# A fused two-layer window-attention kernel: VectorE's order within a slot rewritten, and v taken out of its bank by one operation per half

## What is computed

```python
qkv = (xw @ qkv_w + qkv_b)            # xw: (windows, 64 tokens, 192)
q, k, v = ...                         # 12 heads of 16
attn = softmax(q @ k.T * scale [+ bias + mask])
out = attn @ v                        # per window and head
x = shortcut + unshift(out @ proj_w + proj_b)
x = x + gelu(layernorm(x) @ fc1_w + fc1_b) @ fc2_w + fc2_b
```

## Time and profile before

| | us |
|---|---|
| median of three runs | 4492.06 (4489.7 to 4493.99) |
| the profiled execution, its own time | 4490.49 |
| its span, from first to last instruction | 4488.7 |
| mean granted TensorE clock | 0.904 of 2.4 GHz |
| TensorE matmul busy | 3937.7 (88%) |
| VectorE busy | 3454.4 (77%) |
| GpSimd busy | 3358.2 (75%) |
| ScalarE busy | 2729.8 (61%) |

### The profile page before, as it was taken

The page is one execution under the profiler, slowest core; times in us unless marked ns, Lnnn a source line. Parts: engine busy times, 40 slices in busy tenths (PEclk is TensorE's granted clock), DMA queues, the critical chain, the costliest instruction groups (busy, mean ns, idle before and its releaser), DMA issues. The chain is left out here.

```text
span 4488.7 us, 170135 instructions
## 1 busy us (share of the span) xinstructions
PE 3937.7 (88%) x62800; PEld 2783.4 (62%) x62800; DVE 3454.4 (77%) x9093; ACT 2729.8 (61%) x5921; POOL 3358.2 (75%) x6257
## 2 busy tenths in 40 slices
PE   3888988988999899899889889998998898898888
PEld 2556666666666666666666666666666666666665
DVE  5777777777777777777777777777777777777776
ACT  1566666666666666666666666666666666666665
POOL 4777777777777777777777777777777777777775
PEclk9899998999899899989989998998999899899899
DMA  4877887887788688778867877887787788678775
GB/s 101 148 136 143 143 140 140 141 143 140 138 144 141 137 142 144 136 141 142 142 139 140 142 140 140 141 145 137 143 141 137 142 140 144 141 142 138 135 134 101
DMA packets 2347958, 622.14 MB, mean 139 GB/s; under 512 B 2244598, under 2 KB 2345338, under 8 KB 2347132
## 3 DMA queue, kind: packets, MB, share of 16 engines
q1 hardware_dynamic: 2347132, 611.27, 76.0%
HBM read 32.15 MB, written 25.17 MB: 13 GB/s over the span
## 5 line engine op out<-in xcount | busy, mean ns | idle before, releaser
L1040 POOL TENSOR_TENSOR rstd<-vare,half 128x2 f32<-128x2 f32 x520 | 589.6, 1134 | 663.7 <-DVE vare L877 663.6
L579 PE MATMUL ps_h<-xh,w_fc 128*128 128x512 f16 x3840 | 892.4, 379 | 42.0 <-ACT scaled L700 42.0
L595 PE MATMUL ps_h<-w_fc,hid 128*128 128x192 f16 x9216 | 839.4, 249 | 0.0
L595 PEld LDWEIGHTS ps_h<-w_fc,hid 128*128 128x128 f16 x9216 | 792.4, 100 | 58.1 <-issue 36.5
L685 ACT ACTIVATE stage<-ps_s 128x768 f32<-128x768 f32 x512 | 414.9, 810 | 606.7 <-PE ps_s L537 606.3
L936 DVE TENSOR_TENSOR hid<-scaled,hid 128x512 f16<-128x512 f32 x768 | 668.3, 895 | 143.0 <-POOL hid L1103 136.0
L1103 POOL TENSOR_SCALAR hid<-scaled 128x512 f16<-128x512 f32 x768 | 523.4, 692 | 275.8 <-ACT scaled L700 275.3
L663 ACT ACTIVATE xs<-xn 128x192 f16<-128x192 f32 x512 | 184.6, 361 | 863.6 <-POOL xn L1047 863.6
L579 PEld LDWEIGHTS ps_h<-xh,w_fc 128*128 128x128 f16 x3840 | 361.7, 97 | 485.9 <-ACT scaled L700 154.0
L474 PE MATMUL bank<-w_qkv,xh 128*128 128x384 f16 x2560 | 607.0, 377 | 25.7 <-DMA xh<-xs 13.6
L474 PE MATMUL bank<-w_proj,ot 128*128 128x192 f16 x2560 | 349.6, 276 | 261.2 <-DVE o_tok L916 257.2
(11 more groups left out here) (112 smaller groups left out, 6912.7 us busy)
## 6 DMA issues: line engine op xcount, KB each, us to landing
x_img<-in_x_dram SPq DMA_DIRECT2D x256, 96.0 KB, 2.2
out_dram<-y_img SPq DMA_DIRECT2D x256, 96.0 KB, 2.0
xh<-xs SPq DMA_TRANSPOSE x520, 2.6
qkt<-qk SPq DMA_TRANSPOSE x512, 4.4
pt<-stage SPq DMA_TRANSPOSE x512, 4.1
ot<-os SPq DMA_TRANSPOSE x512, 2.3
stage<-in_L_conv_fc_w_dram SPq DMA_DIRECT2D x2, 384.0 KB, 4.3
stage<-in_L_conv_w_fc_dram SPq DMA_DIRECT2D x2, 384.0 KB, 3.7
```

Of the source, the lines that this page charges most:

```text
L579: last = mm(ps_h[:, u % 2, :].rearrange("p (a t) -> p a t", a=GROUP), w_fc1[layer][:, part, m * 128:(m + 1) * 128], xh[:, p % 2 * GROUP:(p ...
L595: mm(bank[:, 0:C], hid16[:, hs, m, tok], w_fc2[layer][:, ws, m, :], start=(m == 0 and i == 0), stop=False)
L1040: g_.tensor_tensor(rstd[:, m % 2, :], vare[:, m % 2, :], half[:, :].broadcast_to([128, 2]), ALU.pow)\
```

## The change

VectorE's calls in `slot` are put in another order. At place 1 `hidden_lo(2)` and `hidden_lo(3)`, which opened the slot, and `hidden_lo(4)`, which stood ahead of `o_norm`, move behind `row_max`, among the other work of the slot, and `hidden_lo(5)` moves from behind `v_lo` to behind `qk_lo`. At place 0 `v_lo(s)` and `statistics(s+6, 0)` move to directly behind `row_max`, ahead of `attention_residual(s-3)`. The other engines' orders stay as they are.

v of odd heads goes to columns 192 to 383 of `ps_v` in place of 0 to 191. The two blocks that no product writes are set to zero by a `memset` of the whole bank, once for each layer's weights in the set-up, and one operation of 128 x 384 copies both halves, zeros with them, to `v_blk`: one on ScalarE and one on VectorE per tile.

```diff
--- before.py
+++ after.py
@@ -271,11 +271,11 @@
             for s in range(-6, TOTAL + GROUP + 10):
                 slot(s)
 
-        def v_places(n, par, part):
-
-            half = slice(par * 64, par * 64 + 64)
-            src = ps_v[half, 0:C].rearrange("p (e d) -> p e d", d=HD)
-            return src, v_blk[half, n % 2, part, par, :, :, 0:HD].rearrange("p w g d -> p (w g) d")
+        v_sums = ps_v[:, 0:2 * C].rearrange("p (e d) -> p e d", d=HD)
+
+        def v_place(n, part):
+
+            return v_blk[:, n % 2, part].rearrange("p a w g d -> p (a w g) d")[:, :, 0:HD]
 
         o_sums = ps_o[:, 0:HEADS * VW].rearrange("p (h d) -> p h d", d=VW)
 
@@ -499,7 +499,7 @@
                     for w in range(2):
                         for i, (blk, part) in enumerate(((0, 0), (0, 3), (2, 2), (1, 1), (1, 4))):
                             for par in range(2):
-                                last = mm(ps_v[par * 64:par * 64 + 64, w * H2:(w + 1) * H2].rearrange("p (g d) -> p g d", d=HD),
+                                last = mm(ps_v[par * 64:par * 64 + 64, par * C + w * H2:par * C + (w + 1) * H2].rearrange("p (g d) -> p g d", d=HD),
                                           xh[:, n % AHEAD, 0, blk, w * WIN:(w + 1) * WIN],
                                           w_qkv[layer][:, part, 2 * C:3 * C].rearrange("p (g a d) -> p g a d", a=2, d=HD)[:, :, par],
                                           start=(i == 0), stop=(i == 4), skip_group_check=True)
@@ -674,10 +674,7 @@
                 def v_hi(n):
 
                     ge("v_mm", n)
-                    for par in range(2):
-                        src, dst = v_places(n, par, 0)
-                        last = copy(dst, src, ACT.Copy, scale=UNSCALE)
-                    last.then_inc(S["v_hi"], 1)
+                    copy(v_place(n, 0), v_sums, ACT.Copy, scale=UNSCALE).then_inc(S["v_hi"], 1)
 
                 def exp(n):
                     ge("shift", n)
@@ -820,7 +817,8 @@
                 link(v.tensor_copy(qk_bias[:, l, 0, :], row[:, 0:2 * C]))
                 link(v.tensor_tensor(qk_bias[:, l, 1, :], row[:, 0:2 * C], qk_bias[:, l, 0, :], ALU.subtract))
                 link(v.tensor_tensor(vcol[:, 0:1], vcol[:, 0:1], ps_v[:, 0:1], ALU.add))
-                v.tensor_tensor(vcol[0:CB, 1:2], vcol[0:CB, 1:2], ps_v[0:CB, 1:2], ALU.add).then_inc(made, 1)
+                link(v.tensor_tensor(vcol[0:CB, 1:2], vcol[0:CB, 1:2], ps_v[0:CB, 1:2], ALU.add))
+                v.memset(ps_v[:, :], 0.0).then_inc(made, 1)
                 dve.wait_ge(w_in[4 * l + 1], 16 * W_DMAS[1])
                 make_weight(w_proj[l], 1, C, None)
                 dve.wait_ge(folded, 3 * l + 2)
@@ -888,11 +886,8 @@
 
                 def v_lo(n):
                     ge("v_hi", n)
-                    for par in range(2):
-                        src, dst = v_places(n, par, 1)
-                        last = v.scalar_tensor_tensor(out=dst, in0=src, scalar=UNSCALE, in1=v_places(n, par, 0)[1],
-                                                      op0=ALU.mult, op1=ALU.subtract)
-                    last.then_inc(S["v_lo"], 1)
+                    v.scalar_tensor_tensor(out=v_place(n, 1), in0=v_sums, scalar=UNSCALE, in1=v_place(n, 0),
+                                           op0=ALU.mult, op1=ALU.subtract).then_inc(S["v_lo"], 1)
 
                 def row_max(n):
                     ge("s_mm", n)
@@ -938,41 +933,46 @@
 
                 p, place = mlp_phase(s)
                 mlp = 0 <= p < PHASES
-                if mlp and place == 1:
-                    hidden_lo(2)
-                    hidden_lo(3)
+                early = mlp and place == 0
                 if live(s + 5):
                     mean_variance(s + 5, 0)
                 if live(s - 2):
                     inverse_sums(s - 2)
-                if mlp and place == 1:
-                    hidden_lo(4)
-                if live(s - 2):
                     o_norm(s - 2)
                 if live(s):
                     row_max(s)
+                if early and live(s):
+                    v_lo(s)
+                if early and live(s + 6):
+                    statistics(s + 6, 0)
+                if mlp and place == 1:
+                    hidden_lo(2)
                 if live(s - 3):
                     attention_residual(s - 3)
                     statistics(s - 3, 1)
-                if live(s):
+                if live(s) and not early:
                     v_lo(s)
-                if mlp and place == 1:
-                    hidden_lo(5)
                 if live(s - 3):
                     mean_variance(s - 3, 1)
+                if mlp and place == 1:
+                    hidden_lo(3)
                 if live(s + 5) or live(s - 3):
                     centre(s + 5)
-                if mlp and place == 0:
+                if mlp and place == 1:
+                    hidden_lo(4)
+                if early:
                     hidden_lo(0)
                     hidden_lo(1)
                 if live(s):
                     p_lo(s)
                 if live(s + 3):
                     qk_lo(s + 3)
+                if mlp and place == 1:
+                    hidden_lo(5)
                 if mlp and place >= 2:
                     mlp_residual(p * GROUP + 2 * place - 4)
                     mlp_residual(p * GROUP + 2 * place - 3)
-                if live(s + 6):
+                if live(s + 6) and not early:
                     statistics(s + 6, 0)
 
             run(slot)
```

## The result

The changed kernel takes 4388.59 us, the median of four runs (4386.14 to 4391.35), against 4492.16 us before: 103.6 us less, a ratio of 0.977 with a 95% interval of 0.9753 to 0.9787. I had said 4365, with a range from 4258 to 4497. In the middle of the run (groups 17 to 112) a group takes 33.3 us on average, against 34.1 before; I had said 33.1.

The account below looks back on a forecast made before the run. TensorE, busy 88% of the span, was taken as nearest the limit, its loss at places 1 and 2. 4490.5 - 230 + 102 + 1 = 4363.5 us, stated as 4365 because the runs' median lies 1.6 us higher; range 4258 to 4497.

Parts of the forecast that it names:

- `hidden_lo` out of the way: Places 1 and 2: moving `hidden_lo` behind `row_max` brings the shift of place 2 forward 1.8 us per group, 230 us.
- my 4262: Rival at places 1 and 2: the clock stays up and the full 1.8 us is kept, 4262 us; chance 0.15.
- The chain: VectorE's work from `row_max` of place 1 to `row_max` of place 2: 5.92 us before, 8.2 us predicted.
- What TensorE waits for instead: TensorE's moved idle time: about 1.1 us for the exponential, 1.7 for `qk_lo`, up to 0.9 for `o_norm`.
- The clock: Place 2: one MLP output at the low level in half of the groups, costing 0.8 us per group, 102 us.
- two bounds: Low clock's cost at place 2: nothing if it stays up, or 3.1 us more per group for both MLP outputs.
- v, 19 us: v in one VectorE operation saves 0.15 us per tile; only the part inside VectorE's `row_max` to `row_max` stretch counts.
- Place 0 nothing: Place 0: moving `v_lo` and one set of statistics into VectorE's 2.17 us wait for the projection gains nothing.
- memsets 1 us: Set-up: two memsets of a 512-column bank, hidden by nothing, add 1 us in all.
- The clock gives it back in nearly every group: Rival at place 2: the low level costs 1.6 to 1.8 us per group, 4490 or 4470 us; chance 0.20.
- The slower case: Rival at place 2: both MLP outputs run at 1.2 GHz, 3.1 us per group, 4657 or 4560 us; chance 0.08.
- The port rule: VectorE operations with two SBUF inputs and GpSimd's SBUF reads exclude each other: each moved `hidden_lo` 0.95 us, gain 1.4.

Follow-up runs that it names:

- the changed kernel with a full clock: The changed kernel with 3, 6 and 2 unread products per group in TensorE's idle time at places 1 and 2: 4246.01 us, ratio 0.9449.
- the last edits: Changed kernel with `centre` ahead of place 1's `hidden_lo`, and `hidden_lo(4)` and `hidden_lo(5)` behind `row_max` of place 2; with unread products 3, 3, 1: 4201.54 us.
- the last one: Changed kernel with `centre` ahead of place 1's `hidden_lo`, `hidden_lo(4)` and `hidden_lo(5)` behind `row_max` of place 2, no unread products: 4258.14 us, ratio 0.9479.

## Why the prediction was right, and where its terms were off

- **`hidden_lo` out of the way, 230 us at a full clock.** Right in kind and nearly in size, in part by luck: the changed kernel with a full clock is 4246 us, against my 4262. But I had put all of it down to the order. Of the 246 us, 149 are the order's, 24 v's, and 73 the clock that the kernel before had lost already. The chain, 8.2 us predicted, is 7.8; its four `hidden_lo` took 0.98, 1.04, 0.68 and 0.68 us, on average 0.85.
- **What TensorE waits for instead.** `qk_lo` at place 2, as said: 2.15 us, and I had 1.7. The idle time behind the shift is 0.90 us. The wait for `o_norm` at place 2, up to 0.9 us by my account, mostly didn't come: 15 times, 11 us in all. With a full clock it came 66 times but took 20 us, at most 0.4 each. Not seen: the transposes of y behind ScalarE, 100 us in all. I let TensorE come forward and asked only what VectorE would hold it by, not whether GpSimd and ScalarE come forward as well. They do by less: in the groups in question the copy of x is 1.0 us earlier, while `row_max` of place 1 is 2.8 us earlier, since GpSimd's own copies of the next image stand ahead of its norms.
- **The clock, 102 us.** The term that was mis-sized: 142 us measured. I had taken one MLP output at the low level in half of the groups, a choice between two bounds with no row behind it. The first output took more than 1.8 us in 94 of 128 groups, and the outputs together account for 93 us. The other 50 us are not located; the product of q and k ahead of them, which I hadn't priced, took more than 1.2 us (0.99 at 2.4 GHz) in 57 of 125 groups. The gap of 24 us between forecast and result is these 40 us too little for the clock, less the 16 us by which the full-clock time was better than I had said.
- **v, 19 us.** Right at a full clock (24). "Only the part inside the chain counts" is wrong for the time on the chip, where v is worth 48 to 52 us. The step of the prediction that failed here is that v was costed apart from the clock.
- **Place 0 nothing, memsets 1 us.** Both held: 6 us, within the noise, and 0.97 us.
- **The rivals.** "The clock gives it back in nearly every group" describes the sign of what happened, but not its size: it gave back 142 of 246 us. The slower case needed more than 1.8 us per group for the clock; it was 1.1.
- **The port rule.** By the Trainium skill (SBUF — State Buffer, Who interferes with whom) I had each moved operation at 0.95 us in the worst case. Two of the four were near that, and two ran at 0.68 in the same slot. All 768 `hidden_lo` together went from 895 to 835 ns in the mean. So a cost of that size is there, but not in every place; that it comes from GpSimd's reads fits the page and was not tried by itself.

## What to carry to other kernels

When TensorE idles in the same place in every group, price an edit twice: by the chain, and by whether idle time still stands together in one stretch before dense work. The cheapest test is a few unread products in the idle time: here they took 142 us off the changed kernel, more than the 104 of the edit under study, and they separate the two prices of every other edit. Look at the granted clock of such a run: at 0.99 some of the clock's price is still in it. And where an edit brings one engine forward, ask of every other engine that it waits for what stands ahead of its work there. A release that comes earlier (here `centre`, by 2 us) gains little if the engine that it releases is busy with work of its own.

## What the runs showed of the hardware that was not expected

- The value of an edit depended on the clock in both directions. Left alone, it took the order's worth from 149 down to 54 us, v's from 24 up to 48, and that of the last edits from 44 up to 130.
- Unread products of 128x512 in idle time, 11 per group, raised the mean granted clock from 0.936 to 0.997, and the trace puts no wait down to them.
- What exactly makes the level fall was not tried by itself. In the rows shown it fell behind 2.15 us of idle time, with short products ahead of it. The product of q and k at place 2 took more than 1.2 us in 124 of 125 groups of the kernel before, in 57 of the changed kernel and in 37 of the last one, whose longest wait there for `qk_lo` was 1.8 us; more is not shown.
